# A decoder layer on one core: one softmax chunk's shift crosses a body boundary, GpSimd's bias additions get a gate, and one SyncE transfer moves three places down

## The reference

```
att  = softmax(q k^T) over 32 half heads;  diff = att[:16,:16] - lam * att[16:,16:]
f1   = rmsnorm(diff v) * (1 - LAM_INIT) @ Wo^T + bo
f2   = x * scan(decay, ctx * ctx)            # r = decay*r + ctx^2 along the sequence
h    = relu(x @ ternary(W_fc)^T)^2
f3   = rmsnorm(h) @ ternary(W_proj)^T        # hidden width 2048
```

## Time and profile before

| | |
|---|---|
| median of 3 runs | 1143.78 us (1139.13 to 1143.99) |
| profiled execution | 1143.45 us |
| its span | 1141.6 us |
| around the span | 1.85 us |
| TensorE matmul busy | 1047.9 us, 92% of the span |
| VectorE busy | 928.6 us, 81% |
| ScalarE busy | 566.6 us, 50% |
| GpSimd busy | 245.2 us, 21% |
| TensorE's mean granted clock | 0.963 of full speed |

### The profile page before, as it was taken

The page is one execution under the profiler, slowest core; times in us unless marked ns, Lnnn a source line. Parts: engine busy times, 40 slices in busy tenths (PEclk is TensorE's granted clock), DMA queues, the critical chain, the costliest instruction groups (busy, mean ns, idle before and its releaser), DMA issues.

```text
span 1141.6 us, 19562 instructions
## 1 busy us (share of the span) xinstructions
PE 1047.9 (92%) x7008; PEld 826.8 (72%) x7008; DVE 928.6 (81%) x1669; ACT 566.6 (50%) x866; POOL 245.2 (21%) x238
## 2 busy tenths in 40 slices
PE   7999999998999998727989999999999999999994
PEld 5777667676776766515867888878877788888883
DVE  4579898888888998596987998978969969798555
ACT  5442424243434342205556566665663766656672
POOL 6212433434252425131020020020023100200000
PEclk9999999999999999867998999999999999999997
DMA  7977686859596859892120223312202303110011
GB/s 277 306 183 177 144 238 129 247 133 240 134 246 137 213 144 210 239 358 83 38 74 1 74 75 61 112 44 50 106 1 74 111 2 88 61 38 1 1 37 37
DMA packets 167469, 140.50 MB, mean 123 GB/s; under 512 B 140368, under 2 KB 140880, under 8 KB 161488
## 3 DMA queue, kind: packets, MB, share of 16 engines
q1 hardware_dynamic: 96080, 113.83, 36.3%
q10 hardware_dynamic: 71296, 25.43, 9.1%
HBM read 82.61 MB, written 52.95 MB: 119 GB/s over the span
## 4 chain that ended last, share of the span: by engine, by line
PE 61%; DVE 17%; DMA 6%; ACT 6%; issue 5%; SPq 4%; ACTq 1%; DVEq 0%
PE ps_s L804 17%; PE ps_f L788 17%; PE ps_f L615 11%; PE ps_s L632 6%; PE ps_o L740 5%; SPq L432 2%; SPq L402 2%; DVE row_sum L1144 1%; DMA cx<-in_ctx_turned 1%; DMA w_in<-in_fc_turned 1%; DVE cx L1363 1%; DMA w_scr<-w_in 1%; DMA w_raw<-in_qkvo 1%; DMA qbd<-q_scr 1%; ACT f_sb L913 1%
## 5 line engine op out<-in xcount | busy, mean ns | idle before, releaser
L788 PE MATMUL ps_f<-x2h,w 128*128 128x512 f32 x512 | 205.4, 401 | 1.6 <-DVE x2l L1390 1.6
L788 PE MATMUL ps_f<-x2l,w 128*128 128x512 f32 x512 | 201.4, 393 | 0.0
L804 PE MATMUL ps_s<-w,hh 128*128 128x512 f32 x500 | 198.5, 397 | 2.8 <-DVE hl L1398 2.8
L804 PE MATMUL ps_s<-w,hl 128*128 128x512 f32 x500 | 196.5, 393 | 0.0
L615 PE MATMUL ps_f<-xth,wh 128*128 128x512 f32 x376 | 156.6, 416 | 3.4 <-issue 2.7
L1398 DVE TENSOR_TENSOR hl<-h_sb,hh 128x512 fp32r<-128x512 f32 x128 | 93.1, 727 | 81.7 <-ACT hh L1015 81.5
L615 PE MATMUL ps_f<-xtl,wh 128*128 128x512 f32 x376 | 147.8, 393 | 0.0
L615 PE MATMUL ps_f<-xth,wl 128*128 128x512 f32 x376 | 147.7, 393 | 0.0
L632 PE MATMUL ps_s<-qbd,k 128*32 128x128 f32 x2048 | 124.9, 411 | 15.3 <-DMA qbd<-q_scr 15.3
L1595 POOL TENSOR_TENSOR xb<-xb,bob 128x512 f32<-128x512 f32 x32 | 48.8, 1554 | 403.3 <-DMA xb<-in_x 403.3
L632 PEld LDWEIGHTS ps_s<-qbd,k 128*32 128x32 f32 x2048 | 83.0, 147 | 52.4 <-issue 12.8
(11 more groups left out here) (160 smaller groups left out, 1830.7 us busy)
## 6 DMA issues: line engine op xcount, KB each, us to landing
q_scr<-f_sb ACTq DMA_DIRECT2D x32, 256.0 KB, 4.3
k_scr<-f_sb ACTq DMA_DIRECT2D x32, 256.0 KB, 2.7
w_scr<-w_in SPq DMA_DIRECT2D x16, 512.0 KB, 5.8
k<-k_scr SPq DMA_DIRECT2D x8, 1024.0 KB, 8.0
qbd<-q_scr SPq DMA_DIRECT2D x128, 64.0 KB, 4.7
v_scr<-f_sb ACTq DMA_DIRECT2D x32, 256.0 KB, 5.7
ot<-o_scr SPq DMA_DIRECT2D x32, 256.0 KB, 4.6
xb<-in_x SPq DMA_DIRECT2D x8, 1024.0 KB, 5.3
```

The lines of the kernel that those rows point to most:

```text
L788: last = nc.tensor.matmul(ps_f[:, j % 2, :], w1[:, j // 2, k, (j % 2) * P:(j % 2 + 1) * P], xx[:, k, :], start=(k == 0 and xx is x2h), sto ...
L804: last = nc.tensor.matmul(ps_s[:, t, :], a[:, j % 4, t * P:(t + 1) * P], w2[:, j, :], start=(j == 0 and a is hh), stop=(j == HC - 1 and a ...
```

## The change

Three edits. First, `late_shift(3)` leaves step 13 of body 0 on VectorE for the top of body 1, ahead of `late_second(0)`; ScalarE's `exps(3)` that follows it moves from step 14 of body 0 to step 0 of body 1; and `late_second(2)` moves from the top of body 1 to its step 6. Second, GpSimd's four additions in body i wait, besides their data, until TensorE has finished `up(i, 0)`. Third, SyncE issues `o_write(NSB - 2)` after the loads of the context and of `x` for block 1.

```diff
-        LATE_SHIFT = {1: 1, 4: 2, 13: 3}
-        LATE_EXP = {1: 0, 2: 1, 6: 2, 14: 3}
-        LATE_SECOND = {1: (0, 2), 2: (1, 3)}
+        LATE_SHIFT = {1: 1, 4: 2}
+        LATE_EXP = {(0, 1): 0, (0, 2): 1, (0, 6): 2, (1, 0): 3}
+        LATE_SECOND = {1: (0,), 2: (1, 3)}
...
             w1_load(1)
-            o_write(NSB - 2)
             w2_load(1)
             hold((rs_ps, TT))
             cx_load(1)
             hold((x2_done, TT))
             sp.dma_start(xb[:], x_t[1]).then_inc(xb_ld, 16)
+            o_write(NSB - 2)
...
-                    if not later(i) and j in LATE_EXP:
-                        exps(LATE, LATE_EXP[j])
+                    if (i, j) in LATE_EXP:
+                        exps(LATE, LATE_EXP[i, j])
...
                 if not later(i):
                     late_clean(0)
+                if i == 1:
+                    late_shift(3)
                 for c in LATE_SECOND.get(i, ()):
                     late_second(c)
...
                         late_shift(LATE_SHIFT[j])
+                    if (i, j) == (1, 6):
+                        late_second(2)
...
             def body_b(i, prep, fin, ahead):
                 if prep:
+                    pool.wait_ge(f1_ps, at(i, HC, 1))
                     for t in range(TT):
                         add_bias(i + 1, t)
```

## The result

| | before | after |
|---|---|---|
| median of the runs | 1140.27 us (1137.57 to 1143.99, 7 runs) | 1148.57 us (1146.10 to 1151.03, 7 runs) |
| ratio | 1 | 1.007, 95% interval 1.0053 to 1.0087 |
| profiled execution, its span | 1143.45, 1141.6 us | 1151.03, 1149.2 us |
| TensorE, VectorE, GpSimd busy | 1047.9, 928.6, 245.2 us | 1048.8, 931.4, 241.6 us |
| mean granted clock | 0.963 | 0.965 |

The account below looks back on a forecast made before the run. TensorE was taken to bound phase B, with VectorE making its stalls. Costs of 18.65 us against gains of 11.25 gave +7.4 on the profiled 1143.45, so 1150.8 us; range 1138 to 1155, the forecast's own 1147 to 1154.

Parts of the forecast that it names:

- End of body 0: Shift and contention on `hl` and `h_acc` leave VectorE's work there: gain 9.15 us; at body 0's start `otl` waits, cost 0.8.
- D = 2.3 us: VectorE's lateness at a body's start, from additions meeting `hl` and the `hidden_rms` roots, less 0.17 us of idling: 2.3 us.
- Bodies 5 and 6, 1.9 each: At their starts VectorE is 2.3 us late, 0.4 of it covered before TensorE's projection: cost 1.9 us each.
- Body 4, 2.3: VectorE already keeps TensorE waiting 2.8 us for an `hl`, so all of its lateness comes through: cost 2.3 us.
- Body 3, 1.75 less 0.5 at the end: Start: lateness less 0.55 us cover, cost 1.75; end: a smaller `x2l` wait goes as additions leave, gain 0.5.
- Body 2, 5.6 less 1.6 at its end: Start: four additions hold VectorE 4.0 us, clock drop costs 1.6, sum 5.6; end: an `x2l` wait goes, gain 1.6.
- The clock's term: In body 2 the stall of some 4.5 us drops TensorE's clock to 1.2 GHz: cost 1.6 us.
- Body 1, 4.4: Additions against `hl` and roots 3.0, `late_second(2)` at step 6 adds 3.1, cover 1.7, any clock drop inside: cost 4.4 us.
- SyncE's order, nothing: Moving the 1 MB write behind two loads costs nothing, at most 1.7 us; `x` of block 1 lands sooner.
- One turn per body: Rival: at each body's start VectorE loses 1.2 us once, then keeps ahead; net -3.2, 1140.2 us; chance 0.2.
- The gap holds the additions: Rival: additions finish in VectorE's 5.5 us idle stretch at body starts or leave roots unblocked; 1133.6 us; chance 0.17.
- More drops of the clock: Rival: the clock also drops in bodies 5 and 6, +3.2 us, giving 1154.0; chance 0.15.

Follow-up runs that it names:

- that run: The changed kernel with GpSimd's additions of blocks 1 to 7 left out, their signals still sent: 1132.14 us, ratio 0.9932.
- the run with the later gate: The changed kernel with GpSimd's additions waiting for `up(i, 1)` instead of `up(i, 0)`: 1162.02 us, ratio 1.0185.
- the runs with the early gate: Additions wait for the previous body's last `down` but one, none gated in body 0; on the changed kernel: 1133.20 us, ratio 0.9929.
- the run with the sum at step 13: The changed kernel with additions gated on the previous body's last `down` but one, and `late_second(2)` moved from step 6 to 13 of body 1: 1131.10 us.

## Why the prediction was right, point by point

**The whole.** 1150.8 us was forecast from the profiled 1143.45, a difference of 7.4; the two profiled executions differ by 7.58 and the medians by 8.3. The mechanism was right: GpSimd's additions moved off VectorE's last work of a body and onto its first. That the number fits so well is partly luck. Body 1 came out 0.7 dearer than forecast, bodies 2 and 3 came out 0.8 and 0.3 cheaper, and 0.59 of the 7.58 is the later start of phase B, which moves by itself. Of the gain at the end of body 2 one microsecond belongs to the profiled execution alone: the wait for `x2l` there was 1.62 us in it, and 0.60 in the run with SyncE's order alone. The measured median is lower than the forecast because that of before came down from 1143.78 to 1140.27 with more runs.

**End of body 0, 9.15 us less 0.8 at its start:** 8.35 forecast, 8.47 measured. At the start 0.5 came and not 0.8: `otl` took 2.80 us instead of 2.29, and the wait of TensorE that ends 0.1 us after it grew from 2.77 us (before, below) to 3.35; the profile calls it "issue".

```profile
PE ps_o L740 <- issue: 2.8, 1, 2.8
```

`up` of body 1 was looked for at about 602 and came at 602.46. The prediction named both parts, the shift that leaves and the contention that goes with the additions, but not that the whole wait goes only with both: alone the move takes 2.1 us off the 6.4, because two more additions then fall on work that they hold, and the gate takes off 3.2.

**D = 2.3 us:** 2.15 measured. `hl` lost 0.34, L288 0.90 and L290 1.05, against 0.3, 1.0 and 1.15.

**Bodies 5 and 6, 1.9 each:** 1.93 each. The wait is 1.59 us. The other 0.34, which the prediction did not have, is what a wait costs beside itself: L740 starts 1.75 us later than before, counted from L831 (12.67 against 10.92), since the recorded wait begins only when the last matmul's 0.39 us are over, and another 0.18 us goes after it, where the next matmuls start further apart. D was 0.15 smaller and the cover was 0.56 and not 0.4; these errors cancel by luck.

**Body 4, 2.3:** 2.29, by another way. The prediction had all of D come out at the 2.8 us wait of L804. That wait is still 2.80; the loss comes out ahead of it in waits of 0.5 to 0.6 us, at L672 (845.62), at L740 (855.67 and 869.22) and at L760 (880.03).

**Body 3, 1.75 less 0.5 at the end:** 1.25 forecast, 0.92 measured.

**Body 2, 5.6 less 1.6 at its end:** 4.0 forecast, 3.21 measured. VectorE was held 3.65 us and not 4.0 (L1211, L1217, `hl` and L288 lost 0.74, 0.92, 1.09 and 0.90), so L740 waited 3.89 and not 4.5. The clock's term was right:

```profile
698.00:701.00 3.00, 2.92 (x10) 2.31 (x11) 1.27 (x3) 2.94 (x7) 0.00 (x0) 0.75 0.88 101
701.00:704.00 3.00, 3.00 (x11) 2.42 (x10) 2.24 (x5) 0.45 (x1) 0.00 (x0) 0.68 1.08 126
```

(0.25 + 0.32) x 3 = 1.7 us against 1.6.

**Body 1, 4.4:** 5.12 measured, and here a step failed: "a drop of the clock at the first stall is inside that, since VectorE sets the later point". The first wait was 2.05 us and the clock fell; the later wait was 0.98:

```profile
617.00:620.00 3.00, 2.59 (x6) 2.04 (x7) 1.27 (x3) 2.94 (x6) 0.00 (x0) 0.60 0.00 0
620.00:623.00 3.00, 3.00 (x12) 2.41 (x11) 1.98 (x4) 0.79 (x2) 0.00 (x0) 0.84 0.00 0
```

2.05 + 0.98 + 1.7 for the clock + 2 x 0.34 is 5.4, close to the 5.12. The moved softmax steps were too cheap as well: without additions they would cost 1.4 us by the prediction, and cost 2.4 in that run.

**SyncE's order, nothing:** nothing, shown by its own run. That `x` of block 1 "now lands sooner" is not borne out: its transfer was issued 6.23 us before phase B's first L788 in both kernels, and the additions that wait for it began 8.1 to 8.3 us after its issue in the three runs with the old order, and 6.4 to 9.7 us after it in the five with the new one and no gate in body 0, sooner in two and later in three.

**The rivals.** "One turn per body" is refuted by L288 and L290, held one behind the other, and by four in a row in the run with the later gate. "The gap holds the additions" is wrong for this gate and right for one 3.6 us earlier (additions from 3.39 us before L831 instead of 0.24 after it). More drops of the clock: one more than forecast, in body 1; none in bodies 5 and 6. How many there are is not settled by the waits alone, as body 4 of the runs with the early gate showed.

## What to carry to other kernels

Before work of GpSimd is moved, look at VectorE's idle stretches and lay the work so that it ends inside one, not so that it starts there; here 3.6 us of difference in a gate decided between 0.7% slower and 0.7% faster. An edit that empties one place can be worth nothing until the neighbour that fills it is moved too, so try pairs as well as parts. Price the meeting by how many of the other engine's instructions are left at that moment and how long each takes, not by the size of what is held up.

## What the runs showed of the hardware that was not expected

**The turns can be reckoned to about 0.1 us.** The prediction left open which engine goes first. Take GpSimd's instruction as 1.26 us (5.04 / 4). In body 6 the second addition ends at 1000.65 + 2 x 1.26 = 1003.17; `hl` had come at 1002.71 and ends at 1003.74 (1002.71 + 1.03), 0.57 us after that. The third addition was at the head of GpSimd's list from 1003.14 and took 1.75 us instead of 1.26:

```profile
1003.14 1.75 POOL L1599 TENSOR_TENSOR xb<-xb,bob 128x512 f32<-128x512 f32 x1
```

It is reckoned to end at 1003.74 + 1.26 = 1005.00 and ends at 1004.89, L288 at 1004.92, the fourth addition at 1006.14 and L290 at 1006.16: each step of VectorE ends 0.02 to 0.03 us behind the addition that it waited for. So neither engine has a right of way: who has come in the middle of the other's instruction waits for its end and goes next. The case that looked otherwise fits as well. In the kernel before `hl` came at 525.24, just ahead of the third addition's end at 521.59 + 3 x 1.26 = 525.37, and lost nothing that can be seen. After, it came in the middle of one, at 525.83 with the end at 523.91 + 2 x 1.26 = 526.43, and lost 0.5:

```profile
525.83 1.17 DVE L1398 TENSOR_TENSOR hl<-h_sb,hh 128x512 fp32r<-128x512 f32 x1 [4.04 <-ACT hh L1015]
528.73 2.80 DVE L1325 TENSOR_TENSOR otl<-ot,oth 128x2048 fp32r<-128x2048 f32 x1 [1.73 <-ACT oth L979]
```

The Trainium skill (SBUF — State Buffer, section "Who interferes with whom") has the shared port pair taken as an exclusive lock by whichever instruction issues first. The rows agree (`hl`, come at 1002.71, ended only 0.57 us after the addition's end at 1003.17), and add that two engines with more work at hand then alternate.

**What was not held.** The VectorE instructions seen here that read PSUM run on beside the additions. L1421 above took 0.15 us at 1003.66, and in the run with the softmax edits alone the additions ran from 670.85 to 677.34:

```profile
673.17 1.78 DVE L1409 TENSOR_TENSOR h_acc<-h_acc,h_sq 128x512 f32<-128x512 f32 x1
674.87 0.68 DVE L1390 TENSOR_TENSOR x2l<-ps_t,x2h 128x512 fp32r<-128x512 f32 x1
675.47 0.68 DVE L1390 TENSOR_TENSOR x2l<-ps_o,x2h 128x512 fp32r<-128x512 f32 x1
676.40 1.50 DVE L1398 TENSOR_TENSOR hl<-h_sb,hh 128x512 fp32r<-128x512 f32 x1 [0.25 <-ACT hh L1015]
```

One input from PSUM and one from SBUF: 0.68 us each; two from SBUF: 1.78 and 1.50.

**The clock.** The granted clock stayed at full speed (2.4 GHz) after a TensorE wait of 1.59 us (body 6 of the kernel after) and one of 1.60 (body 2 with the early gate), and fell to 0.50 (1.2 GHz) after those of 2.05, 2.21, 3.52 and 3.89 us shown above. The length of a wait does not decide alone: the 2.81 us of body 4 were followed by a fall with the early gate and by none in the run with the sum at step 13, and one of 2.71 us in body 4 of the run with the later gate was followed by none. What does decide is not shown. Each fall shown is 1.7 us, reckoned from the stretches; by body lengths it cost 1.07 in body 4 (80.53 against 79.46), so part of it can be hidden. A wait of 2 us therefore costs here 2.3, itself and 0.34 beside it, and up to 1.7 more where the clock falls.
